# A four-stage image kernel on one Trainium2 core: both input products of a pair of states ahead of both scans

## The reference

```python
def selective_scan(u, delta, A, B, C):
    def step(h, inp):
        u_, de_, b_, c_ = inp
        dA = jnp.exp(de_[..., None] * A)
        h = h * dA + (de_ * u_)[..., None] * b_[:, None, :]
        y = jnp.einsum('bdn,bn->bd', h, c_)
        return (h, y)
...
y = y_f + y_b + y_s
```

## Time and profile before

| | |
|---|---|
| time, median of 3 runs | 768.14 us (762.94 to 768.19) |
| span of the profiled execution | 765.8 us |
| busy in the span: TensorE, weight loads, VectorE, ScalarE, GpSimd | 82%, 47%, 86%, 66%, 59% |
| the six passes, in the span | 301.4 to 615.1 us |
| granted TensorE clock in the passes | 0.84 of full speed |

### The profile page before, as it was taken

One profiled execution on the slowest core, in us unless ns is written; L12 is line 12 of the kernel. 1 busy time (PEld: TensorE's weight loads), 2 busy tenths in 40 slices (PEclk: granted clock), 3 DMA queues, 4 the chain that ended last, 5 costly groups with the idle time before them and its releaser, 6 DMA issues.

```text
span 765.8 us, 11653 instructions
## 1 busy us (share of the span) xinstructions
PE 626.2 (82%) x3947; PEld 359.6 (47%) x3947; DVE 660.8 (86%) x906; ACT 502.1 (66%) x598; POOL 453.1 (59%) x282
## 2 busy tenths in 40 slices
PE   7899999999989933677776778777767789799997
PEld 5655547667764310344453445444534553233332
DVE  7899996889967889999899999998999974788886
ACT  2657512789965868677876877777777710477673
POOL 3798983000001175999999999799899820532321
PEclk9999999999999975689988887899897999899999
DMA  2004100430001030000000000000000004100000
GB/s 56 5 13 103 27 1 12 80 96 8 3 3 58 24 93 17 1 1 0 1 1 0 1 0 1 0 1 1 0 2 0 1 20 80 42 1 1 14 1 14
DMA packets 28853, 14.98 MB, mean 20 GB/s; under 512 B 23022, under 2 KB 24942, under 8 KB 28654
## 3 DMA queue, kind: packets, MB, share of 16 engines
q1 hardware_dynamic: 27582, 13.61, 8.0%
q10 hardware_dynamic: 1216, 0.66, 0.4%
HBM read 5.14 MB, written 0.78 MB: 8 GB/s over the span
## 4 chain that ended last, share of the span: by engine, by line
PE 40%; DVE 37%; ACT 9%; issue 8%; POOL 4%; DVEq 0%; DMA 0%; SPq 0%; ACTq 0%; POOLq 0%
PE ps L572 38%; DVE arena L1380 14%; DVE ps L1053 8%; DVE arena L1053 4%; DVE arena L1099 4%; ACT arena L1620 3%; POOL arena L1781 3%; DVE ps L1099 2%; PE ps L754 1%; ACT arena L1734 1%; DVE arena L1267 1%; ACT x L1734 1%; DVE arena L1331 1%; PE ps L633 1%; ACT arena L1606 1%
## 5 line engine op out<-in xcount | busy, mean ns | idle before, releaser
L572 PE MATMUL ps<-arena 128*32 128x64 f32 (+5 forms) x2072 | 345.5, 357 | 110.7 <-DVE arena L1380 37.1
L572 PEld LDWEIGHTS ps<-arena 128*32 128x32 f32 (+4 forms) x2072 | 125.3, 124 | 245.9 <-issue 97.4
L1781 POOL TENSOR_TENSOR arena<-arena 128x1024 f32<-128x1024 f32 x81 | 188.3, 2337 | 25.6 <-DVE arena L1380 8.5
L1380 DVE TENSOR_TENSOR_SCAN arena<-arena,ps 128x1024 f32<-128x1024 f32 x66 | 150.9, 2287 | 9.0 <-ACT ps L1721 0.5
L1766 ACT ACTIVATE arena<-ps,nycol 128x1024 f32<-128x1024 f32 x64 | 71.1, 1115 | 57.6 <-PE ps L572 57.6
L1053 DVE TENSOR_TENSOR ps<-arena,ps 128x1024 f32<-128x1024 f32 x75 | 90.9, 1212 | 10.0 <-PE ps L572 9.2
L1721 ACT ACTIVATE arena<-arena,a_col 128x1024 f32<-128x1024 f32 x66 | 75.4, 1143 | 16.7 <-DVE arena L1380 16.0
L1902 POOL TENSOR_TENSOR arena<-arena,bmask 128x128 f32<-128x128 f32 x64 | 30.8, 482 | 78.8 <-PE ps L572 67.7
L1053 DVE TENSOR_TENSOR arena<-ps,arena 128x512 f32<-128x512 f32 (+2 forms) x75 | 48.6, 654 | 25.7 <-PE ps L572 20.1
L1380 DVE TENSOR_TENSOR_SCAN arena<-ps,arena 128x1024 f32<-128x1024 f32 x30 | 68.1, 2271 | 2.7 <-POOL arena L1781 2.7
L572 PE MATMUL ps<-ident,arena 128*128 128x128 f32 x416 | 65.9, 312 | 2.0 <-POOL arena L1781 2.0
(11 more groups left out here) (208 smaller groups left out, 1045.8 us busy)
## 6 DMA issues: line engine op xcount, KB each, us to landing
arena<-arena SPq DMA_DIRECT2D x54, 64.0 KB
arena<-arena SPq DMA_DIRECT2D x12, 128.0 KB, 3.3
w_conv<-in_c_far SPq DMA_DIRECT2D x1, 1152.0 KB, 5.7
w_conv<-rpb_pad SPq DMA_DIRECT2D x36, 28.0 KB, 1.8
arena<-x SPq DMA_DIRECT2D x12, 64.0 KB, 2.0
arena<-x1t SPq DMA_DIRECT2D x12, 64.0 KB, 2.0
arena<-x3t SPq DMA_DIRECT2D x12, 64.0 KB, 2.0
arena<-arena SPq DMA_DIRECT2D x2, 288.8 KB, 3.7
```

The source lines that it names most:

```text
L572: return pe.matmul(o, l, r, start=start, stop=stop, **k)
L1380: ve.tensor_tensor_scan(hs_ring[n % RING], decay, add, 0.0, ALU.mult, ALU.add).then_inc(S("scan"), 1)
L1781: return gp.tensor_tensor(o, a, b, ALU.mult)
```

## The change

The set TOGETHER holds the first state of each pair of states that follow each other and both have their product from VectorE. For the SHARED above it is {0, 4, 7, 10, 13}. At such a state VectorE now issues the products of n and n + 1, then the scan of n, then the scan of n + 1; before, it issued product, scan, product, scan. State 2, whose next is shared, stays as it was. The order on all other engines and every wait inside `inject` and `scan` are the same as before.

```diff
+def made_together():
+
+    first, n = set(), 0
+    while n < NS - 1:
+        if n in SHARED or n + 1 in SHARED:
+            n += 1
+        else:
+            first.add(n)
+            n += 2
+    return first
+
+
+TOGETHER = made_together()
...
-                    if n not in SHARED and (k or n):
+                    if n not in SHARED and (k or n) and n - 1 not in TOGETHER:
                         inject(k, n)
+                    if n in TOGETHER:
+                        inject(k, n + 1)
                     scan(k, n)
```

## The result

The changed kernel takes 798.19 us, median of 4 runs (792.68 to 803.7), against 766.71 before, and the ratio is 1.0418 (95% interval 1.0356 to 1.048): 32 us slower. The profiled execution has a span of 793.4 us against 765.8, which is 27.6 more.

A forecast was written before the change was run, and what follows sets the result against it. VectorE's own order was taken to bound the passes. The middle of +30 us (fixed arrivals) and +40 (clock), +35, on the 765.8 us span made 801; with the median 2.3 above the span, 802 was said, range 784 to 826.

The forecast's parts named there:

- What bounds the passes: In the six passes VectorE's own order sets the time, with 12.4 us of stalls and GpSimd 2% behind.
- The handoff, 1.34 to 1.13 us: VectorE start spacing without dependence between neighbours: 0.44 us gained a pair, 13 us at most over 30 pairs.
- S: Start on VectorE of product n, a pair's first product, from which later starts are counted.
- Arrival at S + 2.07 at full clock: The pair's second product can start only then, as TensorE's `b_rep` of n + 1 comes at S + 2.03.
- The losses by place: Fixed arrivals: pairs 4 and 10 lose 24 us, 7 and 13 lose 6.5, pair 0 gains 0.5; sum +30.
- So I keep the arrival R: `b_rep` of n + 1 arrives R after S, unmoved by the new order, which wins only where R is below 1.57.
- The clock: More TensorE idle time brings more half-clock triples (pair plus shared scan): +40 us, granted clock 0.80 or less.
- the 70% forecast: Share of the 24 triples at half clock, 12.3 us each against 9.8 at full: 277 us together, today 237.
- The total: +35 us, the middle between +30 of fixed arrivals and +40 with the clock: 801, stated as 802.
- The waits: VectorE waits for TensorE 24 or more times, 50 to 60 us in sum; GpSimd waits for scans in every triple.
- Rival 3: `b_rep` of n + 1 is there by S + 1.13 and the 13 us are gained: 755 us; chance 0.03.
- Rival 2: TensorE stays at full clock, all 24 triples take 9.8 us: about 765 us, no slower than now; chance 0.06.

The follow-up runs named there:

- run 1: The changed kernel with TensorE sending the spread of B for n + 1 ahead of `b_share` and the collection of n - 4: 753.93 us, ratio 0.9829.
- run 2: TensorE's order as in run 1, but VectorE in the old order (product, scan, product, scan): 761.38 us, ratio 0.9943.
- run 4: The changed kernel with TensorE sending the spread of C of each shared state four times: 780.37 us, ratio 1.0189.
- run 3: The changed kernel with the spread of B for n + 1 behind `b_share` but ahead of the collection: 769.52 us, ratio 1.0038.
- run 8: Run 1 with the spread of C of shared states sent twice: 756.14 us, ratio 0.9877.

## Why the prediction was right, point by point

- **What bounds the passes.** Right. VectorE's own order with little stall: runs 1 and 2 show that its handoffs are worth 8.7 us as soon as no product is late.
- **The handoff, 1.34 to 1.13 us.** Right in size. In the changed kernel a scan follows the second product after 1.14 (453.68 to 454.82); in run 1 the first scan starts 2.24 us behind S (423.57 to 425.81), as 1.13 + 1.12 has it. The Trainium skill's rule (VectorE: DVE Perf Modes, "The DRAIN you can't avoid"), measured there on eight `tensor_copy`, that a semaphore between operations costs nothing would have made runs 1 and 2 equal. They differ by 1.1%, so the measurement decides against it for these operations. No run parts the wait for the semaphore from the dependence on the data: here the two always come together. That the sum would be 13 us higher by the rule was wrong: it holds 0.22 us for each of the 24 late pairs and at most 0.44 for the six pairs 0, so 8 us at most.
- **Arrival at S + 2.07 at full clock.** Right to the hundredth where one collection is in the way, as was the triple of 9.8 us (9.76). Pair 4 of passes 1 and 4 has more ahead of it (S + 4.88 at full clock in run 4). The reason was right too: moving the spread past the two steps in its way took the whole loss and more (run 1), past one of them nearly all of it (run 3).
- **The losses by place.** 24, 6.5 and -0.5 us forecast for pairs 4 and 10, pairs 7 and 13, and pair 0; 18.6, 5.7 and 0.2 measured each by itself. In the changed kernel the places are wrong: 8.7, 21.6 and -0.5. "So I keep the arrival R" held for the sum, 30.3 us in the 24 triples against 30.5, and not for the pairs; that the total still came out is luck.
- **The clock.** That it has a large part was right: run 4 has nine late triples where the changed kernel has 17. That more time would be spent at half clock hardly came true: it was 102 us of the 314 of the passes before and 120 of 342 after, a share of 33% and 35%, and the granted clock fell only from 0.84 to 0.82, not to 0.80. 17 of the 24 triples (71%) were late, which looks like the 70% forecast, but that was a share of triples at half clock throughout, so the likeness is luck. Their arrivals average 3.9 (3.1 to 5.5), where I took R = 4.6 and 12.3 us for each, because the level often falls or rises within the triple. So the 24 triples took 268 us instead of the 277 of that sum. The new order makes a kernel pay for late arrivals that the old one hid: anything between S + 1.57 and S + 3.54 was free before.
- **The total.** +35 was the middle of the two sums, 30 and 40, without a reason for the middle; it was 3 us above the 32 measured. Added up as written, 765.8 + 35 + 2.3 is 803 and not the 802 that I gave.
- **The waits.** 53.4 us in 27 waits, forecast 50 to 60 in 24 or more. GpSimd's waits for scans, 34.9 us in 19 waits (8.5 in 7 before), show the bound moving off it; I had expected one in every triple.
- **The rivals.** Rival 3 (755 us) needed the spread ahead of `b_share` and the transposes. Run 1 made just that and took 754. Rival 2 (765 at full clock) was not reached by run 4 at a clock of 0.94, and its 9.8 us for every triple doesn't hold for pair 4 of passes 1 and 4.

## What to carry to other kernels

Moving an instruction forward on a strictly ordered engine is worth its handoff only if its operand can arrive earlier too: look for the operand's place in the producer's order, not only for the wait that it names. Here a saving of 0.4 us a pair was bought with 0.9 to 4.3 us of waiting, since both scans now stand behind the second product, and the first of them had covered its delay before. Move producer and consumer together: the two edits in one take 754 us, and each alone 761 and 798.

## What the runs showed of the hardware

- A VectorE operation that waits for the semaphore of the one right ahead starts 1.34 us behind a product of 1.21 us; one whose operand is older starts 1.12 to 1.13 behind it. Over 30 pairs this is measurable (8.7 us between runs 1 and 2).
- Repeated, useless matmuls made a kernel faster: 180 more of 96x512 lifted the granted clock of the passes from 0.82 to 0.94 and took 18 us off. A smaller dose (60 more, 0.88 to 0.90) did nothing (756 against 754 us) in run 8, where TensorE was no longer waited for.
- The last pause of TensorE alone doesn't tell at which level the next matmuls run. In the changed kernel four of them took 1.89 us (1.2 GHz) behind the pause of 2.45 us at 437.28, and 1.04 us (2.4 GHz) behind pauses of the same length at two other places, where the level fell only later, within the pair:

```profile
469.09 1.04 PE L587 MATMUL ps<-arena 96*128 96x512 bf16 x4 [2.45 <-DVE arena L1395]
...
503.71 1.04 PE L587 MATMUL ps<-arena 96*128 96x512 bf16 x4 [2.45 <-DVE arena L1395]
```
